# First batch's rows transposed on TensorE, first weights loaded in smaller parts, narrower waits for constants, blank stores moved behind the first turn

## The chip, the cores and the metric

The kernel runs on one core of a Trainium2 chip. The metric is the device time of one execution in microseconds, as the median of several runs. Five engines work side by side, each with its own instruction stream: TensorE (PE; its weight loads are PEld), VectorE (DVE), ScalarE (ACT), GpSimd (POOL) and SyncE (SP), which here mostly issues DMAs. They are ordered among each other only by semaphores that the kernel writes out by hand.

## The reference

For 16 batches of 256 rows of width 512: `x = x + attention(layernorm(x), ctx)`, then `x = x + ffn(layernorm(x))`. The attention is cross attention on 256 context rows of width 256, with 16 query heads and 8 key and value heads of width 128 (`softmax(q k^T / sqrt(128)) v`, then the product with Wo). The ffn works on all 4096 rows at once: a gate picks 4 of 32 experts for a row (2 of 4 groups first), each expert has 128 places and drops what comes after, its output is weighted, and a shared expert (`silu(x Wg) * (x Wu) Wd`) is added for all rows. Everything is float32; the kernel keeps that accuracy by splitting each operand into a float16 high part and a float16 rest and multiplying three times (hi*hi, hi*lo, lo*hi).

## The kernel before, in words

The attention is cut into 128 turns: turn i is batch b = i // 8 and key/value head j = i % 8, which serves two query heads. PE's order is written out in `pe_program`: in turn i it multiplies `scores(i)`, half of `query(i+1)`, `attend(i-1)` (probabilities times values), the other half of `query(i+1)`, `key(i+1)` and `project(i-1)` (product with Wo into ps_out), and in some turns a filler (values of the next batch, gate, rank). So turn 1 is the first with a projection, project(0), at line 1691 with ps_out. After the turns come the experts and the shared expert.

Every product of PE goes through a pair of copies: ACT writes the high half (`query_high`, `key_high`, `value_high`, `head_high`: L905, L899, L912, L1002), then DVE the rest (`query_low`, `key_low`, `value_low`, `head_low`: L1231, L1226, L1237, L1324). Between scores and attend, DVE adds the mask and finds the maxima (`maxima`, L1302), ACT takes the exponentials (`exps`, L989), DVE the scales, POOL and DVE normalise and split them (`probs_high` L734, `probs_low` L1319), and SP turns them by two DMA transposes (`turn_probs`, L570).

Weights are not ready at the start. SP loads them in jobs of up to 512 KB into four staging buffers (`load_weight`, L493); ACT makes the high half (`weight_high`, L893, 128x1024), DVE the rest (`weight_low`, L1170, 128x1024). A buffer is loaded again only after DVE has finished the job before it in that buffer (`next_chunks`). `split_amid` and `split_last` say which jobs are split in which turn, in the middle (behind the maxima) and at the end. A turn takes PE about 9.8 us (project(0) starts at 31.50, project(2) at 51.15 us), and the first turns carry two or three splits each.

The start: SP issues x (two halves), ctx, wk, wq, wv, the mask and two small constants; POOL writes 14 constants (`constants`, L661 to L680), and PE, DVE and ACT all wait for all 14 (`CONSTS`). PE then runs 20 products of zeros (`RAMP`, L1900) to keep itself busy until `key(0)`. Batch 0's layer norm goes DVE statistics (L1174), POOL's inverse deviation (L694), DVE (L1195), ACT's high half (L919), DVE's rest (L1242); SP turns the two row tiles by DMA transpose (L536), and `query(0, h)` waits for both. Behind the transposes on SP stand the next weight loads, the stores of blanks (slot table, blank rows of xn2_rows and of out; L597 to L602) and ctx of batch 1 (L603).

## Time and profile before

| | us |
|---|---|
| median of 3 runs (1606.94 to 1607.52) | 1607.12 |
| the profiled execution, device time | 1609.17 |
| the profiled execution, span of the core | 1607.1 |
| PE busy (share) | 1592.7 (99%) |
| DVE busy | 1221.2 (76%) |
| ACT busy | 843.4 (52%) |
| POOL busy | 787.2 (49%) |
| DMA mean | 137 GB/s |

Matmuls overlap in the profile, so PE's busy time says that it always had one in flight, not that it was at its peak. The start of one matmul to the start of the next is the better measure of its pace.

### The profile page before, as it was taken

What the parts mean: (1) busy time and instruction counts of PE and PEld (TensorE: products, weight loads), DVE (VectorE), ACT (ScalarE), POOL (GpSimd) and SP (SyncE); (2) the same over time, 40 slices, a digit from 0 to 9 for tenths busy, and PEclk for the clock granted to TensorE, in tenths of its full rate; (3) what the DMA queues carried; (4) which work ended last, traced back from release to release, by engine and by line L of the source; (5) the groups of instructions that cost most, each with busy time, mean ns of one, the idle gap of its engine ahead of it and who ended that gap; (6) DMA issues with size and microseconds to landing.
All of it is one profiled execution on the core that took longest, in us unless ns stands there. A gap on an engine that the chain in (4) does not pass through costs nothing. (4 is left out here: it accounts for less than half of the span.)

```text
span 1607.1 us, 36017 instructions
## 1 busy us (share of the span) xinstructions
PE 1592.7 (99%) x12519; PEld 1112.8 (69%) x12519; DVE 1221.2 (76%) x3541; ACT 843.4 (52%) x2086; POOL 787.2 (49%) x1092
## 2 busy tenths in 40 slices
PE   8999999999999999999999999999999999999999
PEld 5666666666666666766666666666677787887876
DVE  7988787878777787878777777878776347776785
ACT  6764544454544554544445454544444156666673
POOL 3444646464555646464645556463536532432432
PEclk9999999999999999999999999999999999999999
DMA  8765445454545454544445444445447658988954
GB/s 256 190 156 120 98 98 109 81 113 80 126 81 126 94 118 97 103 107 100 113 87 126 87 119 100 110 99 104 104 99 260 176 157 244 245 243 261 247 134 95
DMA packets 400243, 219.39 MB, mean 137 GB/s; under 512 B 348464, under 2 KB 356656, under 8 KB 400064
## 3 DMA queue, kind: packets, MB, share of 16 engines
q1 hardware_dynamic: 384176, 191.80, 47.4%
q0 software_dynamic: 15328, 24.25, 8.6%
q8 instruction: 101, 1.65, 0.4%
q10 hardware_dynamic: 560, 1.05, 0.2%
q14 instruction: 78, 0.64, 0.1%
HBM read 92.92 MB, written 40.80 MB: 83 GB/s over the span
## 5 line engine op out<-in xcount | busy, mean ns | idle before, releaser
L989 ACT ACTIVATE arena<-arena,neg_max 128x256 f32<-128x256 f32 x512 | 253.7, 496 | 377.8 <-DVE neg_max L1302 347.5
L734 POOL TENSOR_SCALAR arena<-arena,prob_scale 128x256 f16<-128x256 f32 x384 | 184.6, 497 | 468.5 <-DVE prob_scale L1311 466.4
L1691 PE MATMUL ps_query<-xn_both,arena 128*128 128x256 f16 x1024 | 279.1, 273 | 0.7 <-DMA xn_both<-xn_half 0.7
L1692 PE MATMUL ps_query<-xn_both,arena 128*128 128x256 f16 x1024 | 279.1, 273 | 0.0
L1693 PE MATMUL ps_query<-xn_both,arena 128*128 128x256 f16 x1024 | 279.1, 273 | 0.0
L1302 DVE CUSTOM_DVE_ANT_0 arena<-ps_score,mask_add 128x256 f32<-128x256 f32 x512 | 186.2, 419 | 75.9 <-PE ps_score L1693 74.7
L1319 DVE SCALAR_TENSOR_TENSOR arena<-arena,prob_scale 128x256 f16<-128x256 f32 x384 | 236.3, 664 | 8.5 <-POOL arena L734 8.5
L1691 PE MATMUL ps_out<-arena,o_t 128*128 128x512 f16 x512 | 194.1, 379 | 1.0 <-DVE o_t L1324 1.0
L1692 PE MATMUL ps_out<-arena,o_t 128*128 128x512 f16 x512 | 194.0, 379 | 0.0
L1693 PE MATMUL ps_out<-arena,o_t 128*128 128x512 f16 x512 | 194.0, 379 | 0.0
L1324 DVE SCALAR_TENSOR_TENSOR o_t<-ps_head,o_t 128x512 f16<-128x512 f32 x128 | 88.4, 690 | 97.5 <-ACT o_t L1002 96.0
L784 POOL DMA_INDIRECT slot_table<-entry,slot_at x128 | 130.8, 1022 | 48.0 <-issue 33.8
L1691 PE MATMUL ps_score<-k_both,q_t 128*128 128x256 f16 x512 | 139.5, 272 | 2.8 <-DVE q_t L1231 1.0
L1693 PE MATMUL ps_score<-k_both,q_t 128*128 128x256 f16 x512 | 139.5, 273 | 0.0
L1692 PE MATMUL ps_score<-k_both,q_t 128*128 128x256 f16 x512 | 139.5, 272 | 0.0
L1002 ACT ACTIVATE o_t<-ps_head 128x512 f16<-128x512 f32 x128 | 76.1, 594 | 88.9 <-PE ps_head L1826 65.5
L1691 PEld LDWEIGHTS ps_query<-xn_both,arena 128*128 128x128 f16 x1024 | 100.2, 98 | 26.3 <-DMA xn_both<-xn_half 1.2
L1692 PEld LDWEIGHTS ps_query<-xn_both,arena 128*128 128x128 f16 x1024 | 100.2, 98 | 25.2
L1439 DVE SCALAR_TENSOR_TENSOR arena<-arena 128x1024 f16<-128x1024 f32 x96 | 116.1, 1220 | 0.1
L1693 PEld LDWEIGHTS ps_query<-xn_both,arena 128*128 128x128 f16 x1024 | 100.2, 98 | 11.5
L1014 ACT ACTIVATE arena<-arena 128x1024 f16<-128x1024 f32 x96 | 100.7, 1049 | 2.2 <-PE ps_out L1693 2.2
L742 POOL TENSOR_TENSOR arena<-arena 128x256 f16<-128x256 f32 x128 | 91.7, 717 | 10.7
(343 smaller groups left out, 4175.5 us busy)
## 6 DMA issues: line engine op xcount, KB each, us to landing
arena<-w SPq DMA_DIRECT2D x96, 512.0 KB, 5.4
x_in<-x SPq DMA_DIRECT2D x15, 512.0 KB, 3.7
out_rows_dram<-x SPq DMA_DIRECT2D x30, 256.0 KB, 2.4
xn_rows<-xn_half SPq DMA_DIRECT2D x15, 512.0 KB
out_rows_dram<-weight_in POOLq DMA_DIRECT2D x28, 256.0 KB
x2t_kept<-xn_both SPq DMA_DIRECT2D x12, 512.0 KB, 3.0
ctx_in<-ctx_t SPq DMA_DIRECT2D x16, 256.0 KB, 3.0
weight_in<-wq SPq DMA_DIRECT2D x8, 512.0 KB, 5.0
```

The source lines that it names most:

```text
L734: pool.tensor_scalar(p_rows[:, 0, c, :], probs[:, c, :], prob_scale[:, c:c + 1], 1.0, ALU.mult, ALU.mult).then_inc(norm_hi, 1)
L742: pool.tensor_tensor(p_rows[:, 1, c, :], probs[:, c, :], p_rows[:, 0, c, :], ALU.subtract).then_inc(last_lo, 1)
L784: pool.indirect_dma_start(slot_table, bass.IndirectOffsetOnAxis(ap=slot_at[z % 2][:, t, k:k + 1], axis=0), entry[z % 2][:, t, k, :], None, ...
L989: act.activation(probs[:, c, :], probs[:, c, :], ACT.Exp, bias=neg_max[:, c:c + 1], scale=-1.0, accum_out=prob_sum[:, c:c + 1]).then_inc(e ...
L1014: act.activation(expert_w[e % HELD].hi[:, at], expert_in[e % AHEAD][:, at], ACT.Copy, scale=W_S).then_inc(expert_hi[part], 1)
L1302: dve.tensor_tensor_reduce(out=probs[:, c, :], in0=ps_score[h][:, t * S:(t + 1) * S], in1=mask_add[b % 2][:, :], scale=-SCORE_SCALE, scala ...
L1319: dve.scalar_tensor_tensor(p_rows[:, 1, c, :], probs[:, c, :], prob_scale[:, c:c + 1], p_rows[:, 0, c, :], ALU.mult, ALU.subtract).then_in ...
L1324: dve.scalar_tensor_tensor(o_t.lo, ps_head[:, :], 1.0 / P_S, o_t.hi, ALU.mult, ALU.subtract).then_inc(head_lo, 1)
L1439: dve.scalar_tensor_tensor(expert_w[e % HELD].lo[:, at], expert_in[e % AHEAD][:, at], W_S, expert_w[e % HELD].hi[:, at], ALU.mult, ALU.sub ...
L1691: pe.matmul(dst, a.hi, b.hi, start=start and n == 0, stop=False)
L1692: pe.matmul(dst, a.hi, b.lo, start=False, stop=False)
L1693: m = pe.matmul(dst, a.lo, b.hi, start=False, stop=stop and n == len(pairs) - 1)
```

## The change

`first_transposed(t)` transposes row tile t of batch 0 on PE: 8 transposes of 128x128 against a float16 identity (`ident_first`, a view of o_t that POOL fills, one memset and one select more) into the two score banks as float16. ACT's `first_copy(0)` and DVE's `first_copy(1)` bring them to xn_both. The two DMA transposes of batch 0 go. The first loads are six jobs without a wait: Wq's first two heads in two jobs of 128 columns, Wk's first head of 128 columns, wv, wq chunk 1, the rest of Wk; later jobs move by two in number. ACT waits for 2 constants, PE for 1, 8 and then all, DVE for all only ahead of turn 0, where POOL's memset of xn2_half and minus_half come first. PE runs 16 products of zeros, then 3 and 4 behind the two transposed tiles, then query(0), key(0), value(0,0,0); value(0,0,1) goes behind key(1). ACT and DVE take query(1) and key(1) ahead of the normalising in turn 0, split three jobs (5, 6 and 7) in turn 0 in place of two, and take ctx of batch 1 in turn 1 (POOL) and turn 2 (DVE). SP issues the load of job 7 (wo 0) only after DVE's split of job 5, and ctx(1) and the blank stores behind the probabilities' transposes of turn 0.

```diff
@@ -66,8 +66,8 @@
-RAMP = 20
-RAMP_KEY = 3
+RAMP = 16
+RAMP_TURNED = (3, 4)
@@ -225,6 +225,7 @@
...
         spare_row = sbuf("spare_row", [1])
+        ident_first = o_t.hi[:, 0:P]
@@ -346,7 +349,8 @@
-        CONSTS = 14
+        CONSTS = 16
+        PLAIN_CONSTS = 7
@@ -363,15 +367,18 @@
...
-        jobs = [by_columns("wk", wk_s, wk, KC, 0, 512, 0), by_columns("wq", wq_s, wq, KD, 0, 256, 1),
-                by_columns("wv", wv_s, wv, KC, 0, 512, 2), by_columns("wq", wq_s, wq, KD, 1, 256, 3),
-                by_columns("wq", wq_s, wq, KD, 2, 256, 0), by_rows("wo", wo_s, wo, PAIR, D, 0, 1),
+        rest = slice(HD, 512)
+        jobs = [by_columns("wq_first", wq_s, wq, KD, 0, HD, 1), by_columns("wq_first", wq_s, wq, KD, 1, HD, 1),
+                by_columns("wk_first", wk_s, wk, KC, 0, HD, 0), by_columns("wv", wv_s, wv, KC, 0, 512, 2),
+                by_columns("wq", wq_s, wq, KD, 1, 256, 3),
+                (("wk", 0), wk_s[:, :, rest], rows_of(wk)[:, :, rest], KC, 512 - HD, 0),
+                by_columns("wq", wq_s, wq, KD, 2, 256, 1), by_rows("wo", wo_s, wo, PAIR, D, 0, 0),
                 by_columns("wv", wv_s, wv, KC, 1, 512, 2), by_columns("wq", wq_s, wq, KD, 3, 256, 3),
-                by_rows("wo", wo_s, wo, PAIR, D, 1, 0), by_columns("wk", wk_s, wk, KC, 1, 512, 1)]
+                by_rows("wo", wo_s, wo, PAIR, D, 1, 1), by_columns("wk", wk_s, wk, KC, 1, 512, 0)]
...
@@ -380,10 +387,14 @@
...
+        FIRST_LOADS = 6
+        beside_another = {1: KD * HD, 5: KC * HD}
+
+        split_amid = {0: (6,), 1: (8,), 2: (11,), 3: (14,), 4: (16,), 5: (18,), 6: (20,), 7: (21,), 8: (24,), 9: (26,),
+                      10: (27,)}
+        split_last = {0: (7,), 1: (9, 10), 2: (12, 13), 3: (15,), 4: (17,), 5: (19,), 6: (22, 23), 8: (25,), 10: (28,)}
@@ -391,7 +402,14 @@
...
             _, _, _, rows, cols, buf = jobs[n]
-            return weight_in[buf // 2][:, buf % 2 * 1024:][:, 0:rows * cols].rearrange("p (k n) -> p k n", k=rows)
+            at = buf % 2 * 1024 + beside_another.get(n, 0)
+            return weight_in[buf // 2][:, at:at + rows * cols].rearrange("p (k n) -> p k n", k=rows)
+
+        def weight_landed(n):
+            if n < len(in_begin):
+                return in_begin[n], 16
+            uses_of_it = [m for m in same_buffer(n) if m >= len(in_begin)]
+            return in_weight[jobs[n][5]], 16 * (uses_of_it.index(n) + 1)
@@ -487,10 +505,10 @@
...
             def load_weight(n):
-                earlier_one = [m for m in same_buffer(n) if m < n]
-                if earlier_one:
+                if n >= FIRST_LOADS:
+                    earlier_one = [m for m in same_buffer(n) if m < n]
                     sp.wait_ge(weight_lo, earlier_one[-1] + 1)
-                sp.dma_start(weight_buf(n), jobs[n][2]).then_inc(in_weight[jobs[n][5]], 16)
+                sp.dma_start(weight_buf(n), jobs[n][2]).then_inc(weight_landed(n)[0], 16)
@@ -582,29 +600,28 @@
...
+            def blank_stores():
+                sp.wait_ge(consts, CONSTS)
+                sp.dma_start(slot_table.rearrange("(p e) c -> p (e c)", e=E),
+                             blank[:, :, :].rearrange("p e c -> p (e c)")).then_inc(out_blank, 16)
+                sp.dma_start(xn2_rows[N:N + CAP, :], xn2_half[:, 0, :, :].rearrange("p h d -> p (h d)")).then_inc(out_blank, 16)
+                for n in range(2):
+                    sp.dma_start(out[N + n * CAP:N + (n + 1) * CAP, :],
+                                 xn2_half[:, 0, :, :].rearrange("p h d -> p (h d)").bitcast(F32)).then_inc(out_blank, 16)
...
             load_x(0)
+            for n in range(2):
+                load_weight(n)
             load_ctx(0)
-            for n in range(3):
+            for n in range(2, FIRST_LOADS):
...
             sp.dma_start(bias_row[:, :], gate_bias.broadcast_to([P, E])).then_inc(in_const, 16)
-            for t in range(TB):
-                turn_xn(0, t)
-            load_weight(3)
-            next_chunks((0, 1, 2))
...
-            load_ctx(1)
-
+            next_chunks((1, 3, 4, 5))
...
                 b, j = divmod(i, KV)
-                next_chunks(split_last.get(i - 1, ()) if i else (3,))
+                next_chunks(split_last.get(i - 1, ()))
@@ -617,6 +634,9 @@
...
                 turn_probs(i)
+                if i == 0:
+                    load_ctx(1)
+                    blank_stores()
@@ -658,13 +678,16 @@
...
             def constants():
+                pool.memset(xn2_half[:, 0, :, :], 0.0).then_inc(consts, 1)
+                pool.memset(minus_half[:, :], -0.5).then_inc(consts, 1)
+                pool.memset(ident_first, 0.0).then_inc(consts, 1)
...
                 pool.memset(lower[:, :, :], 1.0).then_inc(consts, 1)
-                pool.memset(xn2_half[:, 0, :, :], 0.0).then_inc(consts, 1)
                 pool.memset(blank[:, :, 1], 0).then_inc(consts, 1)
-                pool.memset(minus_half[:, :], -0.5).then_inc(consts, 1)
-                pool.wait_ge(consts, 6)
+                pool.wait_ge(consts, PLAIN_CONSTS)
+                pool.affine_select(out=ident_first, in_=ident_first, compare_op=ALU.not_equal, fill=1.0, base=0,
+                                   pattern=[[-1, P]], channel_multiplier=1).then_inc(consts, 1)
@@ -818,7 +841,7 @@
...
                 probs_high(i)
-                if i == 0:
+                if i == 1:
@@ -889,7 +912,7 @@
...
             def weight_high(n):
-                act.wait_ge(in_weight[jobs[n][5]], 16 * (same_buffer(n).index(n) + 1))
+                act.wait_ge(*weight_landed(n))
@@ -926,6 +949,11 @@
...
+
+            def first_copy(t):
+                act.wait_ge(pe_first, t + 1)
+                act.activation(xn_both[0][:, :, :, t * P:(t + 1) * P], ps_last[t].rearrange("p (h k c) -> p h k c", h=2, k=KD),
+                               ACT.Copy, scale=1.0).then_inc(first_copied, 1)
@@ -1054,27 +1082,30 @@
...
-            act.wait_ge(consts, CONSTS)
+            act.wait_ge(consts, 2)
...
                 xn_high(0, t)
-            for n in (0, 1):
+            weight_high(0)
+            first_copy(0)
+            for n in (1, 2, 3):
                 weight_high(n)
+            query_high(0)
             key_high(0)
-            weight_high(2)
-            query_high(0)
-            weight_high(3)
+            for n in (4, 5):
+                weight_high(n)
+            act.wait_ge(consts, CONSTS)
...
                 if i == 0:
-                    for n in split_amid[0]:
-                        weight_high(n)
+                    value_high(ps_fill[0], 0, 0, 0)
...
                 if i == 0:
-                    value_high(ps_fill[1], 0, 0, 0)
+                    query_high(1)
+                    key_high(1)
@@ -1084,15 +1115,17 @@
                 if i == 0:
+                    for n in split_amid[0]:
+                        weight_high(n)
...
@@ -1262,6 +1295,11 @@
...
+            def first_copy(t):
+                dve.wait_ge(pe_first, t + 1)
+                dve.tensor_copy(xn_both[0][:, :, :, t * P:(t + 1) * P], ps_last[t].rearrange(
+                    "p (h k c) -> p h k c", h=2, k=KD)).then_inc(first_copied, 1)
@@ -1485,23 +1523,25 @@
...
-            dve.wait_ge(consts, CONSTS)
...
                 xn_rest(0, t)
+            weight_low(0)
+            first_copy(1)
+            weight_low(1)
             ctx_low(0)
-            for n in (0, 1):
+            for n in (2, 3):
                 weight_low(n)
+            query_low(0)
...
                 value_scaled, 1)
+            weight_low(4)
             dve.wait_ge(value_scaled, 1)
-            weight_low(2)
-            query_low(0)
-            weight_low(3)
+            dve.wait_ge(consts, CONSTS)
@@ -1511,7 +1551,10 @@
...
                     maxima(i)
-                for n in split_amid.get(i, ()):
+                if i == 0:
+                    weight_low(5)
+                    value_low(ps_fill[0], 0, 0, 0)
+                for n in split_amid.get(i, ()) if i else ():
@@ -1542,7 +1585,8 @@
...
                 if i == 0:
-                    value_low(ps_fill[1], 0, 0, 0)
+                    query_low(1)
+                    key_low(1)
@@ -1552,16 +1596,13 @@
...
-                if i == 0:
-                    query_low(i + 1)
-                    key_low(i + 1)
@@ -1571,7 +1612,10 @@
...
                 if i == 0:
+                    for n in split_amid[0]:
+                        weight_low(n)
                     value_low(ps_fill[0], 0, 0, 1)
+                if i == 2:
@@ -1695,11 +1739,14 @@
...
                 b, g = divmod(i, KV)
-                if h == 0:
-                    pe.wait_ge(xt_turned, 16 * TB * (b + 1))
-                    pe.wait_ge(weight_lo, prepared["wq", g])
-                    if i:
-                        pe.wait_ge(query_lo, i)
+                if i == 0:
+                    pe.wait_ge(first_copied, TB)
+                    pe.wait_ge(weight_lo, prepared["wq_first", h])
+                elif h == 0:
+                    if b:
+                        pe.wait_ge(xt_turned, 16 * TB * b)
+                    pe.wait_ge(weight_lo, prepared["wq", g] if g else prepared["wq_first", 1])
+                    pe.wait_ge(query_lo, i)
@@ -1709,7 +1756,7 @@
...
                 pe.wait_ge(ctx_lo, b + 1)
-                pe.wait_ge(weight_lo, prepared["wk", g // 4])
+                pe.wait_ge(weight_lo, prepared["wk", g // 4] if i else prepared["wk_first", 0])
@@ -1720,6 +1767,13 @@
...
+
+            def first_transposed(t):
+                pe.wait_ge(xn_lo, t + 1)
+                for n in range(2 * KD):
+                    h, k = divmod(n, KD)
+                    m = pe.transpose(ps_last[t][:, n * P:(n + 1) * P], xn_half[:, t, h, k * P:(k + 1) * P], ident_first)
+                m.then_inc(pe_first, 1)
@@ -1894,24 +1948,28 @@
...
-            pe.wait_ge(consts, CONSTS)
+            def ramp(count):
+                for _ in range(count):
+                    pe.matmul(ps_out[0][:, :], zeros[:, 0:P], zeros, start=True, stop=True)
+
+            pe.wait_ge(consts, 1)
             zeros = xn2_half[:, 0, 0, :]
-            for _ in range(RAMP):
-                pe.matmul(ps_out[0][:, :], zeros[:, 0:P], zeros, start=True, stop=True)
-            key(0)
-            for _ in range(RAMP_KEY):
-                pe.matmul(ps_out[0][:, :], zeros[:, 0:P], zeros, start=True, stop=True)
+            ramp(RAMP)
+            pe.wait_ge(consts, PLAIN_CONSTS + 1)
+            for t in range(TB):
+                first_transposed(t)
+                ramp(RAMP_TURNED[t])
...
                 query(0, h)
+            key(0)
+            pe.wait_ge(consts, CONSTS)
...
                 if i == 0:
-                    filler(("value", 0, 0, 0), ps_fill[1])
+                    filler(("value", 0, 0, 0), ps_fill[0])
...
                     scores(i)
-                if i == 0:
-                    filler(("value", 0, 0, 1), ps_fill[0])
@@ -1926,6 +1984,8 @@
...
                     key(i + 1)
+                if i == 0:
+                    filler(("value", 0, 0, 1), ps_fill[0])
```

## Rows read from the trace of the kernel before

**Rows 1.** Waits of PE from 31 us on: total us, times, longest.
```profile
PE ps_out L1691 <- DVE o_t L1324: 1.0, 3, 0.6
```
**Rows 2.** Busy time by stretch: PE, PEld, DVE, ACT, POOL; PEclk, DMA share, GB/s.
```profile
31.40:60.00 28.60, 28.50 (x191) 18.57 (x192) 27.20 (x63) 21.13 (x48) 15.48 (x20) 1.00 0.84 237
...
400.00:1190.00 790.00, 788.47 (x5713) 534.03 (x5712) 625.44 (x2052) 392.89 (x1124) 423.88 (x624) 1.00 0.48 104
```
**Rows 3.** Timeline of the start: start us, us, engine, line, operation [idle before <-releaser].
```profile
3.72 1.28 DVE L1174 BATCH_NORM_STATS2 stats<-x_in 128x6 f32<-128x512 f32 x2 [3.72 <-POOL blank L680]
...
3.74 6.70 PE L1900 MATMUL ps_out<-xn_half 128*128 128x512 f16 x20 [3.74 <-POOL blank L680]
...
6.51 0.95 DVE L1195 TENSOR_SCALAR x<-x_in,mean_var,rstd 128x512 f32<-128x512 f32 x1 [1.22 <-POOL rstd L694]
...
8.15 1.29 DVE L1242 SCALAR_TENSOR_TENSOR xn_half<-x,xn_half 128x512 f16<-128x512 f32 x2 [0.24 <-ACT xn_half L919]
...
8.87 2.72 SPq L536 DMA_TRANSPOSE xn_both<-xn_half  x2
...
11.33 0.27 PE L1691 MATMUL ps_fill<-ctx_both,arena 128*128 128x256 f16 x1 [0.89 <-DVE arena L1170]
...
13.49 0.28 PE L1691 MATMUL ps_query<-xn_both,arena 128*128 128x256 f16 x1 [0.70 <-DMA xn_both<-xn_half]
```
**Rows 4.** Loads issued at 0.81, 11.64 and 12.84 us: KB, us from issue to landing.
```profile
x_in<-x SPq DMA_DIRECT2D x1, 256.0 KB, 2.6
...
weight_in<-wq SPq DMA_DIRECT2D x1, 512.0 KB, 3.8
...
weight_in<-wo SPq DMA_DIRECT2D x1, 512.0 KB, 6.4
```
**Rows 5.** Timeline of turns 0 and 1.
```profile
16.32 0.60 ACT L905 ACTIVATE q_t<-ps_query 128x512 f16<-128x512 f32 x1 [2.81 <-PE ps_query L1693]
...
17.70 0.28 PE L1691 MATMUL ps_score<-k_both,q_t 128*128 128x256 f16 x1
...
19.04 0.42 DVE L1302 CUSTOM_DVE_ANT_0 arena<-ps_score,mask_add 128x256 f32<-128x256 f32 x1
...
25.02 0.27 PE L1691 MATMUL ps_score<-k_both,q_t 128*128 128x256 f16 x1 [1.04 <-DVE q_t L1231]
...
26.50 1.21 DVE L1170 SCALAR_TENSOR_TENSOR arena<-weight_in,arena 128x1024 f16<-128x1024 f32 x1
...
27.64 0.41 DVE L1302 CUSTOM_DVE_ANT_0 arena<-ps_score,mask_add 128x256 f32<-128x256 f32 x1
...
30.75 0.69 DVE L1324 SCALAR_TENSOR_TENSOR o_t<-ps_head,o_t 128x512 f16<-128x512 f32 x1 [0.17 <-ACT o_t L1002]
...
31.50 0.39 PE L1691 MATMUL ps_out<-arena,o_t 128*128 128x512 f16 x1 [0.16 <-DVE o_t L1324]
```
**Rows 6.** By line: ns min/median/max, first and last start; one row of the timeline.
```profile
L1021 ACT ACTIVATE xn_both<-ps_fill x32: 1001/1012/1024, 1294.1 to 1573.0; 128x1024 f16<-128x1024 f16 x32
...
L1170 DVE SCALAR_TENSOR_TENSOR arena<-weight_in,arena x20: 1209/1215/1418, 10.0 to 85.7; 128x1024 f16<-128x1024 f32 x20
...
L1216 DVE TENSOR_SCALAR weight_in<-x,mean_var,rstd x4: 531/540/628, 1146.7 to 1211.5; 128x512 f32<-128x512 f32 x4
...
1214.76 1.06 PE L1728 MATMUL ps_score<-blank,xn_half 128*128 128x128 f16 x16
```
**Rows 7.** Turn 3 in the timeline, and DVE's waits for PE from 31 to 110 us.
```profile
49.92 0.69 DVE L1324 SCALAR_TENSOR_TENSOR o_t<-ps_head,o_t 128x512 f16<-128x512 f32 x1
...
51.15 0.38 PE L1691 MATMUL ps_out<-arena,o_t 128*128 128x512 f16 x1
...
DVE arena L1302 <- PE ps_score L1693: 2.0, 2, 1.3
```
**Rows 8.** Busy time by stretch within the products of zeros, columns as in Rows 2.
```profile
3.70:8.30 4.60, 4.56 (x11) 1.64 (x12) 3.08 (x7) 1.01 (x3) 1.53 (x3) 1.00 1.01 339
8.30:10.50 2.20, 2.14 (x10) 0.78 (x8) 2.20 (x4) 2.20 (x3) 0.00 (x0) 1.00 0.60 168
```

More of the change, by code:

```diff
@@ L307, in build @@
         in_weight = [signal(f"in_weight{n}") for n in range(4)]
+        in_begin = [signal(f"in_begin{n}") for n in range(3)]
+        pe_first, first_copied = signal("pe_first"), signal("first_copied")
         xt_turned, x2t_turned, out_rows, out_xn2, in_table = (signal(n) for n in ("xt_turned", "x2t_turned", "out_rows", "out_xn2", "in_table"))
@@ L381, in build @@
         prepared = {job[0]: n + 1 for n, job in enumerate(jobs)}
-        split_amid = {0: (4,), 1: (6,), 2: (9,), 3: (12,), 4: (14,), 5: (16,), 6: (18,), 7: (19,), 8: (22,), 9: (24,),
-                      10: (25,)}
-        split_last = {0: (5,), 1: (7, 8), 2: (10, 11), 3: (13,), 4: (15,), 5: (17,), 6: (20, 21), 8: (23,), 10: (26,)}
-        assert sorted(n for table in (split_amid, split_last) for ns in table.values() for n in ns) == list(range(4, JOBS))
+        FIRST_LOADS = 6
[3 more added lines that the diff above has]
+        split_last = {0: (7,), 1: (9, 10), 2: (12, 13), 3: (15,), 4: (17,), 5: (19,), 6: (22, 23), 8: (25,), 10: (28,)}
+        assert sorted(n for table in (split_amid, split_last) for ns in table.values() for n in ns) == list(
+            range(FIRST_LOADS, JOBS))
         def same_buffer(n):
@@ L415, in build @@
         before = {}
-        for bank_no, first_use in ((0, [("value", 0, 0, 1)]), (1, [("key", 0), ("value", 0, 0, 0)])):
+        for bank_no, first_use in ((0, [("value", 0, 0, 0), ("value", 0, 0, 1)]), (1, [("key", 0)])):
             held = list(first_use)
@@ L591, in sync_program @@
             sp.dma_start(bias_row[:, :], gate_bias.broadcast_to([P, E])).then_inc(in_const, 16)
-            for t in range(TB):
-                turn_xn(0, t)
-            load_weight(3)
-            next_chunks((0, 1, 2))
-            sp.wait_ge(consts, CONSTS)
-            sp.dma_start(slot_table.rearrange("(p e) c -> p (e c)", e=E),
-                         blank[:, :, :].rearrange("p e c -> p (e c)")).then_inc(out_blank, 16)
-            sp.dma_start(xn2_rows[N:N + CAP, :], xn2_half[:, 0, :, :].rearrange("p h d -> p (h d)")).then_inc(out_blank, 16)
-            for n in range(2):
-                sp.dma_start(out[N + n * CAP:N + (n + 1) * CAP, :],
-                             xn2_half[:, 0, :, :].rearrange("p h d -> p (h d)").bitcast(F32)).then_inc(out_blank, 16)
-            load_ctx(1)
+            next_chunks((1, 3, 4, 5))
             for i in range(TURNS):
                 b, j = divmod(i, KV)
-                next_chunks(split_last.get(i - 1, ()) if i else (3,))
+                next_chunks(split_last.get(i - 1, ()))
                 if j == 1 and b + 1 < B:
@@ L1563, in dve_program @@
                 early_key = live and second(b, j) is not None and second(b, j)[0] == "value"
-                if i + 1 < TURNS and early_key:
+                if 0 < i < TURNS - 1 and early_key:
                     key_low(i + 1)
```

10 lines of the change are left out of this document (5 added, 5 removed).

## The prediction

> **What bounds the kernel now.** I read the waits of PE first, then the busy time by stretch, then the timeline of the first 52 us. PE is the bound from its first projection on: between 400 and 1190 us it is busy for 788.47 of 790 us [rows 2], and from 31 us to the end its largest wait, for o_t, sums to 1.0 us in three places [rows 1]. So the end moves by what project(0), at 31.50 us [rows 5], moves, less any new stall behind it. What lies ahead of 31.50 is a start-up whose waits aren't covered. PE begins real work with key(0) at 11.33 and query(0) at 13.49 [rows 3]. A product of 256 columns starts every 0.109 us, one of 512 every 0.216, so PE's own work up to project(0) is 16.33 us: key and query(0) 3.27, two values 2.6, two scores 2.62, query(1) 2.62, key(1) 0.65, query(2) 2.62, attend(0) 1.3, key(2) 0.65. From 11.33 to 31.50 it takes 20.17, so 3.84 us are holes (1.5 ahead of query(0), filled with three products of zeros, 1.2 ahead of scores(1), the rest small).
>
> DVE is the hidden second bound. From 26.50 to 31.50 its instructions stand back to back, with 0.17 us of idle [rows 5], and between 31.4 and 60 it is busy for 27.20 of 28.60 [rows 2]. project(0) waits for DVE's o_t (30.75 + 0.69), that for ACT behind exps(1), and exps(1) for maxima(1) at 27.64 [rows 5]. Moving PE's start alone would thus be worth nothing; DVE's chain must move too.
>
> **The change part by part.** All times are of the profiled execution.
>
> Constants. DVE's statistics waited for POOL's last constant at 3.72 [rows 3]; the first half of x had landed at 0.81 + 2.6 = 3.4 [rows 4], but the second, issued 0.46 later and 0.3 slower, only at about 4.2, where DVE stood at 4.3 anyway. The wait was nearly hidden: worth 0.1. POOL's two more constants (about 0.4, ending at 4.1) lie ahead of the statistics' end at 5.2, so they cost nothing; without that cover, 0.4. PE starts its zeros at about 1.8 and ends them near 7.5; its wait for x follows.
>
> Layer norm. DVE's first L1195 took 0.95 beside POOL's split of ctx, where the same shape otherwise takes 0.54 [rows 3, 6]. ctx now comes behind two weight loads, at about 7.8, so I take 0.54. The normalised rows end at 6.9 and 7.4, ACT's high halves at 7.6 and 8.1, DVE's rests at 8.3 and 8.9 (0.61 apart, as in [rows 3]).
>
> Transposes. Removed: 8.87 to 13.49, that is two issues of 1.36 one after the other and the landing [rows 3]. Added: 8 transposes per tile, 0.45 us (16 stand in 0.89 [rows 6]); tile 0 from 8.4, the zeros behind it 0.64, tile 1 from 9.5 to 10.0. ACT's copy takes 1.01 [rows 6] and ends at 10.0. DVE's copy of 128x1024 float16 out of PSUM has no row. The nearest are 1.22 for a two-input operation with 1024 elements and 0.54 for a one-input one with 512 [rows 6]; I take 1.2 by equal element count and keep 0.6 as the lower end. It runs from 10.15 to 11.35, so query(0) starts at 11.42, against 13.49. ACT's splits of 512 and 256 elements lie beside it, and all the small loads have landed by then.
>
> The Trainium skill, "VectorE: DVE Perf Modes", section "Why PSUM operands drop a tier", says that an operand in PSUM still allows two 16-bit elements a cycle in a one-input operation. By that rule the copy takes about 0.6 (an estimate) and the sum ends 0.55 us lower. No row here shows it.
>
> Turn 0, from query(0) at 11.42. Query ends at 14.04, key(0) at 14.7 (ctx and Wk's head are split at 12.9), value(0,0,0) at 16.0 (wv split by DVE at 14.1). ACT and DVE bring q_t and k_t as before, 0.3 and 0.6 us behind PE's last product [rows 5]: ready at 15.96, hidden by the value, so scores(0) starts at 16.0 against 17.70. DVE's split of job 4 ends at 17.45, which holds query(1) by 0.2, and maxima(0) start at 17.4 against 19.04. Then DVE: maxima 1.38, job 5 (768 elements) 0.87, value 0.67, scales 0.45, done at 20.65; q_t and k_t of turn 1 follow ACT, which follows PE's query(1) at 20.1 and key(1) at 20.8: ready at 22.0. PE covers this with value(0,0,1) until 22.07, so scores(1) starts at 22.07 against 25.02. DVE goes on with three rests of the probabilities to 23.35, job 6 (1.14) to 24.5, value to 25.2, job 7 (1.14) to 26.35. The chain from query(0) to maxima(1) has no slack of DVE over 0.7 us: maxima(1) start at 26.35 against 27.64. PE does query(2) from 24.6 (held 1.2 by job 6's split), attend(0) at 26.15 and its last third at 27.45 (the probabilities' second transpose), and ends key(2) at 29.86.
>
> Turn 1, as before from maxima(1): exps(1) end at 28.8, o_t's high half at 29.4, DVE's rest at 29.42 + 0.69, project(0) at 30.16. PE's own account gives the same: 16.33 of work and 2.4 of holes from 11.42. **Gain at project(0): 1.34.**
>
> Job 7 (wo 0) was loaded at 12.84 and now waits for the split of job 5, so it is issued at 19.7. With 3.8 us on a quiet queue, as the load at 11.64 had [rows 4], it lands at 23.5, is split by ACT by 24.6 and costs nothing. The margin is 0.7 us.
>
> Turns 1 to 3. ctx(1), the blank stores (0.8 MB) and ctx's splits stood under start-up holes of SP and in turn 0 of DVE. On SP they now stand ahead of the load of wo 1, which is issued at 28.3 instead of 26.93; it lands near 32.3, and ACT wants it by 32.65. DVE's ctx split (0.61) moves from turn 0 to turn 2. So DVE is 1.34 ahead in turns 1 and 2 but 0.73 in turn 3, while PE is 1.34 ahead. There o_t was ready at 49.92 + 0.69 and used at 51.15, slack 0.54 [rows 7]: 0.61 of it goes, and PE stalls by about 0.1. Later DVE waits for PE twice, up to 1.3 us [rows 7], so it catches up and nothing more is lost. Wait for a late wo 1: 0 to 0.8, taken as 0.1.
>
> **Sum.** 1.34 - 0.1 - 0.1 = 1.1 us. The profiled span of 1607.1 goes to 1606.0; the median of the runs shown is 1607.12, equal to that span though the profiled execution's device time was 1609.17, so I take the same 1.1 off the median: 1606.0.
>
> **The rivals.**
> Rival 1, the copy is fast: everything from query(0) on starts 0.55 earlier, 1605.5. For it, the row with one input is fast for its size [rows 6]; against it, that row is from SBUF. This is the page's rule, above.
>
> Rival 2, the weights come late and it ends slower than before. The place is the load of wo 0 and, behind it, wo 1. Their landing times range from 3.8 to 6.4 [rows 4]. Landing of wo 0 after 19.7 + 5.7 = 25.4 puts maxima(1) behind 27.64 (1.05 for ACT, 1.14 for DVE, and hand-overs), and the gain is gone; at 6.4 it is 26.1, project(0) at 32.2, and the time 1607.9. For it: no cover left on DVE. Against: only one other load (wq 3, issued at 17.5) is under way then.
>
> Rival 3, the clock. In the first 4.60 us of zeros 11 products of 512 columns start (0.42 us each, the lower level, 1.2 GHz), in the next 2.20 us 10 (0.22, the upper, 2.4 GHz) [rows 8]. PE then held the upper level through holes of 0.9 and 0.7 us [rows 3]. Now there is a hole of 0.9 ahead of the transposes, and transposes with zeros in place of key(0). If the lower level is granted there, transposes and zeros take 1.4 more up to query(0), and query(0) 2.6 more: 1606.0 + 4.0 = 1610.0. Against it: the 16 transposes at 1214.76 ran 0.056 apart, the upper level [rows 6], though between dense products.
>
> The Trainium skill, "TensorE: Matmul & The Clock Gate", section "Part 4: PE-mode transpose", says that the full clock doesn't engage for transposes, since they don't count as busy in the same way. By that rule rival 3 would be likely; the trace agrees only that they can run at the upper level.
>
> Rival 4, the stall is hidden anyway: DVE stays as late as before through its added split in turn 0, PE only waits longer for o_t, and the time is 1607.1. For it: DVE's work in turn 0 grows by 0.87 (job 5) less 0.61 (ctx). Against: its chain starts 1.64 earlier.
>
> **How the numbers follow.** Forecast 0.43 (1605.6 to 1606.5), rival 1 0.20, rival 2 0.12, rival 3 0.06, rival 4 0.15, and 0.04 for a gain beyond this: with no hole at all and the fast copy, project(0) would come at 27.2 and the time be 1602.8. About 0.2% (3.2 us) is what a measurement of this kernel can tell from no change. Nearly every case lies within it: same 0.92, faster 0.03, slower 0.05. The range is 1604.6 to 1607.9; it holds all but parts of rival 3, the large gain and a late load.
>
> **What would show it.** Right: query(0) near 11.4 with its transposes 0.056 apart; scores(0) near 16.0 and scores(1) near 22.1; maxima(1) near 26.4; project(0) near 30.2; a stall of about 0.1 at project(2). L1170 for wo 0 without idle time ahead of it. Wrong: transposes 0.107 apart (rival 3), DVE idle ahead of job 7 or 10 (rival 2), maxima(1) at 27.6 (rival 4), a DVE copy of 0.6 (rival 1), or PE stalls behind turn 3 larger than before.

## The result and the profile after

The changed kernel takes 1611.67 us (median of 9 runs, 1610.38 to 1613.86) against 1607.21 for the kernel before in the same comparison (9 runs): a ratio of 1.0028, 95% interval 1.002 to 1.0037. It is slower, by about 4.5 us, where 1.1 us of gain was forecast. The profiled execution took 1612.24 us with a span of 1610.4, which is 3.3 more than the 1607.1 of before. The rest of the 4.5 didn't come back: in later comparisons the kernel before took 1608.83 to 1609.27 and the changed one 1611.89, so the loss to be explained is 3.1 to 3.3 us.

The start came nearly as forecast. L1775 are the transposes on TensorE, L955 and L1300 the two copies. This is the timeline of the changed kernel up to project(0) (start us, us, engine, line, operation, idle before and releaser):

```profile
1.81 5.48 PE L1953 MATMUL ps_out<-xn_half 128*128 128x512 f16 x16 [1.81 <-POOL minus_half L682]
...
6.43 1.00 DVE L1228 TENSOR_SCALAR x<-x_in,mean_var,rstd 128x512 f32<-128x512 f32 x2 [1.22 <-POOL rstd L717]
...
8.92 0.61 PE L1775 MATMUL ps_score<-o_t,xn_half 128*128 128x128 f16 x8 [1.63 <-DVE xn_half L1275]
...
9.56 1.02 ACT L955 ACTIVATE xn_both<-ps_score 128x1024 f16<-128x1024 f16 x1 [0.88 <-PE ps_score L1775]
...
10.01 0.61 PE L1775 MATMUL ps_score<-o_t,xn_half 128*128 128x128 f16 x8
...
10.65 0.69 DVE L1300 COPY xn_both<-ps_score 128x1024 f16<-128x1024 f16 x1 [0.68 <-PE ps_score L1775]
...
11.40 0.28 PE L1735 MATMUL ps_query<-xn_both,arena 128*128 128x256 f16 x1
...
16.03 0.27 PE L1735 MATMUL ps_score<-k_both,q_t 128*128 128x256 f16 x1
...
25.02 0.28 PE L1735 MATMUL ps_query<-xn_both,arena 128*128 128x256 f16 x1 [1.36 <-DVE arena L1203]
...
26.68 0.41 DVE L1340 CUSTOM_DVE_ANT_0 arena<-ps_score,mask_add 128x256 f32<-128x256 f32 x1
...
30.54 0.39 PE L1735 MATMUL ps_out<-arena,o_t 128*128 128x512 f16 x1 [0.60 <-DVE o_t L1362]
```

project(0) is 0.96 us earlier than the 31.50 of [rows 5]. The loss lies behind it. Busy time by stretch (PE, PEld, DVE, ACT, POOL; granted clock, DMA share, GB/s), the same stretches as [rows 2]:

```profile
31.40:60.00 28.60, 24.52 (x166) 15.81 (x165) 24.55 (x57) 17.15 (x37) 10.51 (x17) 1.00 0.85 218
400.00:1190.00 790.00, 788.81 (x5717) 535.20 (x5716) 627.79 (x2049) 396.05 (x1125) 427.05 (x626) 1.00 0.49 104
```

Between 400 and 1190 us nothing differs. Between 31.4 and 60 PE is busy for 24.52 us instead of 28.50, so 3.98 us go missing there. Two holes hold them, shown in PE's timeline:

```profile
38.23 0.38 PE L1875 MATMUL ps_head<-arena 128*128 128x512 f16 x1 [2.31 <-DMA arena<-arena]
54.49 0.39 PE L1735 MATMUL ps_out<-arena,o_t 128*128 128x512 f16 x1 [1.77 <-DVE o_t L1362]
```

The first is attend(1), which waits for SP's transposes of the probabilities of turn 1. The second is project(2). Before, neither wait existed [rows 1, 7]. The waits between 28 and 110 us (total, times, longest) tell what is behind the second:

```profile
ACT arena L916 <- DMA weight_in<-wq: 4.4, 1, 4.4
...
DVE arena L1203 <- ACT arena L916: 2.6, 2, 2.0
...
PE ps_out L1735 <- DVE o_t L1362: 2.4, 2, 1.8
PE ps_head L1875 <- DMA arena<-arena: 2.3, 1, 2.3
ACT arena L916 <- DMA weight_in<-wo: 2.0, 1, 2.0
```

ACT waits 4.4 us for one load of Wq (columns of turn 5, job 14); DVE, which works in order, can't go on to turn 2's o_t without it. SP's timeline tells why this load and the transposes are late. First the kernel before:

```profile
24.28 2.60 SPq L570 DMA_TRANSPOSE arena<-arena  x2
26.93 0.58 SPq L493 DMA_DIRECT2D weight_in<-wo  x1
...
32.85 2.85 SPq L570 DMA_TRANSPOSE arena<-arena  x2
35.76 0.57 SPq L493 DMA_DIRECT2D weight_in<-wq  x1
36.38 0.53 SPq L493 DMA_DIRECT2D weight_in<-wo  x1
36.95 0.47 SPq L493 DMA_DIRECT2D weight_in<-wq  x1
41.58 3.05 SPq L570 DMA_TRANSPOSE arena<-arena  x2
```

And the changed one:

```profile
22.77 2.73 SPq L588 DMA_TRANSPOSE arena<-arena  x2
25.54 0.58 SPq L532 DMA_DIRECT2D ctx_in<-ctx_t  x1
26.17 0.48 SPq L605 DMA_DIRECT2D slot_table<-blank  x1
26.68 0.43 SPq L607 DMA_DIRECT2D xn_rows<-xn_half  x1
...
28.14 0.54 SPq L511 DMA_DIRECT2D weight_in<-wo  x1
...
31.88 5.03 SPq L588 DMA_TRANSPOSE arena<-arena  x2
...
41.28 3.66 SPq L588 DMA_TRANSPOSE arena<-arena  x2
45.00 1.62 SPq L511 DMA_DIRECT2D weight_in<-wq  x2
```

Two things are to be seen. The two transposes of turn 1 begin at 31.88, earlier than before, but take 5.03 us to issue instead of 2.85, behind ctx(1), the blank stores and the loads queued after them. I call this cause Q (queue). And the third load of turn 2, issued at 36.95 before, is now issued at 45.00, behind the transposes of turn 2. A buffer is loaded again only after DVE has split the job before it there. The change exchanges buffers 0 and 1 for the first twelve jobs, while the later ones keep theirs. Before, that Wq load took the buffer of wo 1, split at the end of turn 1; now it takes the buffer of Wk's second half, split in the middle of turn 2. Wo's chunk for turn 3 took that late buffer before, where it did no harm, since it is split at the end of turn 3, and the Wq load already in the middle of it. I call this cause B (buffers).

### The profile page after: what moved, and what is told of

The parts are those of the page before. It is cut to its first block, busy times and chain, and to the rows that moved or that the text cites. A ratio compares the mean times of both kernels' runs of the same rounds, so it can differ in the third digit from the quotient of the medians.

```text
span 1610.4 us, 36059 instructions
## 1 busy us (share of the span) xinstructions
PE 1593.2 (99%) x12535; PEld 1113.9 (69%) x12535; DVE 1226.9 (76%) x3544; ACT 849.5 (53%) x2089; POOL 789.0 (49%) x1094
## 4 chain that ended last, share of the span: by engine, by line
PE 92%; DVE 2%; DMA 2%; issue 1%; SPq 1%; POOL 1%; ACT 0%; POOLq 0%; DVEq 0%
PE ps_query L1735 8%; PE ps_query L1737 8%; PE ps_query L1736 8%; PE ps_fill L1737 7%; PE ps_fill L1736 7%; PE ps_fill L1735 7%; PE ps_out L1735 7%; PE ps_out L1736 7%; PE ps_out L1737 7%; PE ps_score L1735 5%; PE ps_score L1737 5%; PE ps_score L1736 5%; PE ps_head L1880 3%; PE ps_head L1875 3%; PE ps_head L1876 3%; PE ps_fill L1902 1%
## 5 line engine op out<-in xcount | busy, mean ns | idle before, releaser
L807 POOL DMA_INDIRECT slot_table<-entry,slot_at x128 | 130.2, 1017 | 48.0 <-issue 33.8
L1875 PE MATMUL ps_head<-arena 128*128 128x512 f16 x256 | 96.9, 378 | 2.3 <-DMA arena<-arena 2.3
```

The source lines that it names most:

```text
L807: pool.indirect_dma_start(slot_table, bass.IndirectOffsetOnAxis(ap=slot_at[z % 2][:, t, k:k + 1], axis=0), entry[z % 2][:, t, k, :], None, ...
L1875: pe.matmul(ps_heads, v.hi, p_t[s].hi, start=s == 0, stop=False)
```

## The experiments

What the runs are compared by, beside the ratio, is the start of project(i) in the profiled execution less that of the kernel before, in us:

| run | project(0) | (1) | (2) | (3) | end | ratio to before (95%) |
|---|---|---|---|---|---|---|
| the change | -0.96 | +1.40 | +3.34 | +3.45 | +3.26 | 1.0028 (1.002 to 1.0037) |
| e12, the change again | -0.99 | +1.44 | +2.43 | +2.54 | +3.57 | 1.0018 (1.0008 to 1.0027) |
| e1 blank stores early | -0.35 | -0.46 | +1.88 | +3.58 | +3.74 | 1.0015 (1.0006 to 1.0024) |
| e2 buffers as before | -1.29 | +2.44 | +2.44 | +2.44 | +4.05 | 1.0015 (1.0006 to 1.0024) |
| e3 both | -0.12 | -0.23 | +0.23 | +0.34 | -0.37 | 1.0006 (0.9997 to 1.0015) |
| e4 before, blanks late | -0.04 | +0.83 | +0.83 | +0.83 | +0.26 | 1.0007 (0.9998 to 1.0016) |
| e5 both, ctx(1) early too | +1.06 | +0.96 | +1.42 | +1.53 | +1.86 | 1.0016 (1.0007 to 1.0025) |
| e6 buffers, blanks in turn 4 | -1.42 | -1.53 | -1.26 | -1.10 | +0.24 | 0.9997 (0.9988 to 1.0006) |
| e11, the same again | -1.25 | -1.33 | -1.11 | -0.13 | +0.14 | 0.9997 (0.9988 to 1.0006) |
| e7 e6, rows turned by DMA | +3.50 | +3.70 | +3.70 | +3.84 | +4.18 | 1.0037 (1.0023 to 1.005) |
| e8 e6, all constants waited for | +0.10 | +0.21 | +0.67 | +0.78 | +0.65 | 1.0004 (0.9995 to 1.0014) |
| e9 blanks in turn 4 alone | -1.53 | -1.63 | +0.67 | +0.87 | +0.76 | 1.0011 (1.0002 to 1.0021) |
| e10 before, buffers exchanged | +0.31 | +0.28 | +2.64 | +2.75 | +3.16 | 1.0018 (1.0009 to 1.0027) |

One profiled execution is good to about 1 us here: the change and e12 are one kernel and differ by 0.9 at project(3), e6 and e11 by 1.0 (e11 has one more wait of 0.71 at attend(3) for turned probabilities). Ratios of about 1.0015 with intervals of 0.0009 to each side can hardly be told from one another, so the waits in the traces carry the argument on the single causes. The times forecast for the first runs were set against 1607.2, while the kernel before took 1609.05 beside e1 to e4.

**e1, the blank stores ahead of wo 0.** Undoes most of Q alone.

```diff
-            next_chunks((1, 3, 4, 5))
+            next_chunks((1, 3, 4))
+            blank_stores()
+            next_chunks((5,))
...
                 if i == 0:
                     load_ctx(1)
-                    blank_stores()
```

> The changed kernel with one thing undone: the blank stores (0.8 MB) are issued in the start-up again, ahead of the load of wo 0; ctx of batch 1 stays behind the transposes of turn 0. Theory Q (queue): the stores, issued at 26.2 to 28.1 us, push the loads behind them, and these the probabilities' transposes of turn 1, for which attend(1) waits 2.31 us. 0.8 MB at 350 GB/s is 2.3 us, so that wait falls to under 0.5 and the time to 1609.0 to 1610.0. Theory B (buffers): the stall comes from the staging buffers' exchange; the wait at attend(1) stays above 1.5 and the time within 0.5 of 1611.7.

The wait at attend(1) is gone, as theory Q has it; the time of 1611.88 is above its forecast. For project(0) keeps only 0.35 of its gain, and project(2) waits 1.96 (B, untouched). Then the clock falls: project(3) comes another 1.70 late. Busy time by stretch in e1:

```profile
51.00:53.00 2.00, 0.07 (x1) 0.00 (x0) 1.90 (x8) 1.41 (x5) 0.66 (x2) 1.00 0.00 0
53.00:55.00 2.00, 1.97 (x8) 0.84 (x9) 2.00 (x4) 2.00 (x5) 1.92 (x4) 0.79 0.00 0
55.00:57.00 2.00, 2.00 (x6) 0.68 (x5) 2.00 (x4) 1.01 (x2) 1.71 (x4) 0.50 0.68 129
```

After 2 us in which PE is busy for 0.07, the granted clock falls to 0.50 (1.2 of 2.4 GHz) for the work that follows. In this execution the hole cost more than its length.

**e2, the buffers exchanged back.** Undoes B alone: in the first twelve jobs 0 and 1 change places, as in the kernel before.

```diff
-        jobs = [by_columns("wq_first", wq_s, wq, KD, 0, HD, 1), ...
+        jobs = [by_columns("wq_first", wq_s, wq, KD, 0, HD, 0), ...
```

> The changed kernel with staging buffers 0 and 1 exchanged for the first twelve jobs, so that wo 1 lies in buffer 0 and Wk's second half in buffer 1, as before the change. Theory B: wq chunk 5 (buffer 0) is loaded again at the start of turn 2 and not behind its transposes; ACT's wait of 4.4 us for it in turn 3 and DVE's of 2.0 go, and PE's stall of 1.77 at project(2) falls to under 0.5: 1609.5 to 1610.3. Theory Q: project(2) is late only because attend(1) was; exchanging buffers changes nothing, 1611.7 within 0.5.

ACT's wait of 4.4 for wq and the wait at project(2) go, as theory B has it; the one at attend(1) stays, at 2.01. The time, 1611.09, is above the forecast. Yet project(1) moves by 3.73 from project(0), since here too the clock falls after the hole:

```profile
35.00:37.00 2.00, 0.59 (x6) 0.28 (x3) 2.00 (x8) 1.68 (x4) 0.24 (x1) 1.00 1.18 198
...
39.00:41.00 2.00, 2.00 (x11) 1.37 (x10) 1.03 (x3) 0.99 (x2) 1.72 (x5) 0.50 0.95 319
```

So 1.7 of e2's 3.73 are clock (3.73 - 2.01). The changed kernel itself had a hole of 2.31 (2.38 in e12) at the same place and its clock stayed at 1.00 in both profiled executions. Of all fourteen profiles only e1, e2 and e7 show a 2 us stretch below 0.99. The fall of the clock doesn't explain why undoing one cause alone brought so little in the medians: the mean granted clock of a whole execution is 0.999 in 2 of e1's 11 executions and in 3 of e2's 11, and 1.000 in the others, whose medians are 1611.01 and 1611.03. It is 0.999 in 3 of the first 9 executions of the changed kernel too, in 3 of e10's 11 and in none of e12's 10.

**e3, both together,** the edits of e1 and e2:

```diff
+            blank_stores()
...
+        jobs = [by_columns("wq_first", wq_s, wq, KD, 0, HD, 0), ...
```

> Both edits: blank stores in the start-up and the first twelve jobs' buffers exchanged. If theories Q and B each hold a part, both stalls go and only the gain of 0.96 at project(0) is left, less small waits: 1606.0 to 1607.0, faster than the kernel before by 0.2 to 1.2. If only Q holds: as the first run of this call. If only B: as the second.

Both waits go, the span (1606.7) lies in the forecast and the ratio's interval holds 1. But the start gain, which the forecast kept, is lost: project(0) comes at 31.38. In the timeline of e3 ACT waits for wo 0 (issued at 19.83 behind the blank stores):

```profile
25.28 2.00 ACT L917 ACTIVATE arena<-weight_in 128x1024 f16<-128x1024 f32 x2 [2.42 <-DMA weight_in<-wo]
```

**e4, the kernel before with its blank stores behind turn 0's transposes.** Q's main part alone, nothing else of the change.

```diff
-            [the four blank stores, in the start-up]
...
                 turn_probs(i)
+                if i == 0:
+                    [the four blank stores]
```

> The kernel before with one part of the change alone: the blank stores are issued behind the probabilities' transposes of turn 0 (ctx of batch 1 stays where it was). Theory Q: the loads of turn 1 and the transposes of turn 1 land later; PE waits 1 to 2 us at attend(1): 1608.0 to 1609.5. Theory B: no buffer changes, so nothing happens: 1607.2 within 0.3.

A wait of 0.82 appears at attend(1), under the 1 to 2 us expected, and project(1) to project(3) come 0.83 later, at full clock:

```profile
37.66 0.38 PE L1822 MATMUL ps_head<-arena 128*128 128x512 f16 x1 [0.82 <-DMA arena<-arena]
```

This isolates the blank stores' part in Q. It is smaller than 2.31. Two things differ from the changed kernel, and no run tells them apart: ctx(1) isn't in the queue here, and the transposes of turn 1 begin at 32.80 and not at 31.88 (they take 3.46 to issue). The ratio doesn't tell it from no change.

**e5, e3 with ctx(1) early too,** so that nothing of the change's late traffic is left.

```diff
             next_chunks((1, 3, 4))
+            load_ctx(1)
             blank_stores()
```

> As the version with both edits (blank stores in the start-up, first twelve jobs' buffers exchanged), but ctx of batch 1 is loaded in the start-up too, ahead of the stores. Theory Q: 0.25 MB less stands ahead of turn 1's loads; but 1.05 MB now stand ahead of wo 0, which already held maxima(1): project(0) comes at 31.4 to 31.9 against 31.50 before the change, no stall in turns 1 to 3, span 1606.9 to 1607.6. Rival (the start-up's gain is real whatever the stores do): project(0) at 30.2 to 30.5 and span near 1606.

Worse than e3, and than expected (project(0) at 32.56 against 31.4 to 31.9): ACT waits 3.5 for wo 0, attend(0) waits 1.54 for its turned probabilities, project(0) is 1.06 later than before. The place in front of wo 0 isn't free at all: wo 0 is issued at 20.69 and lands 5.8 later, against 19.75 and 3.7 in the changed kernel.

**e6, buffers as before and the blank stores behind turn 4's transposes.**

```diff
                 if i == 0:
                     load_ctx(1)
+                if i == 4:
                     blank_stores()
```

> The changed kernel with the first twelve jobs' buffers exchanged and the blank stores issued behind the transposes of turn 4 (ctx of batch 1 behind those of turn 0). Theory Q: nothing stands ahead of wo 0 or of turn 1's loads but ctx; project(0) stays at 30.2 to 30.5, the wait at attend(1) is under 0.3, project(3) is 0.8 to 1.3 us earlier than in the kernel before, and the span is 1605.8 to 1606.4: faster than before by 0.05 to 0.08%. Rival (ctx of batch 1 alone is enough to delay the transposes of turn 1): attend(1) waits over 1 us and the span is 1607 or more.

Both holes are gone with the start gain kept, as expected: -1.42 at project(0), -1.10 at project(3). The span was forecast at 1605.8 to 1606.4 and is 1607.3; this is taken up at the end. SP's timeline of e6, against that of the changed kernel:

```profile
31.41 2.61 SPq L588 DMA_TRANSPOSE arena<-arena  x2
34.08 0.57 SPq L511 DMA_DIRECT2D weight_in<-wq  x1
34.70 0.52 SPq L511 DMA_DIRECT2D weight_in<-wo  x1
35.27 0.47 SPq L511 DMA_DIRECT2D weight_in<-wq  x1
```

The transposes take 2.61 again, and job 14 is issued at 35.27, not 45.00. Against before the median is 1608.66 to 1609.27, which is no difference that can be told.

**e9, the blank stores in turn 4 with the change's buffers,** and **e10, the kernel before with buffers 0 and 1 exchanged in its ten written-out jobs.** These two isolate B.

```diff
                 if i == 0:
                     load_ctx(1)
+                if i == 4:
                     blank_stores()
```

```diff
-        jobs = [by_columns("wk", wk_s, wk, KC, 0, 512, 0), by_columns("wq", wq_s, wq, KD, 0, 256, 1),
+        jobs = [by_columns("wk", wk_s, wk, KC, 0, 512, 1), by_columns("wq", wq_s, wq, KD, 0, 256, 0),
...
```

> The changed kernel with the blank stores issued behind turn 4's transposes and its own buffers kept (wo 1 in buffer 1, Wk's second half in buffer 0). Theory Q predicts no wait at attend(1); theory B predicts that the late load of wq chunk 5 still holds project(2) and project(3): 1.8 to 3.5 us together, so project(3) at +0.7 to +2.5 against the kernel before. If B were only a consequence of the queue's delay, project(3) would be at -1.1 as in the version with exchanged buffers.

> The kernel before with one part of the change alone: staging buffers 0 and 1 exchanged for the first ten jobs, the later ones as they were. Theory B: wq chunk 5 is loaded behind turn 2's transposes, ACT waits 4 to 5 us for it in turn 3 and PE is later by 2.5 to 3.7 us from project(3) on; ratio 1.0015 to 1.0023. Rival (the order of buffers costs only where the start-up is early already): under 0.5 us.

In e9 there is no wait at attend(1), although ctx(1) still stands there, so Q doesn't come about without the blank stores. From project(1) to project(2) it loses 2.30. SP's timeline of e9 shows both, quick transposes in turn 1 and the late Wq load:

```profile
31.32 2.63 SPq L588 DMA_TRANSPOSE arena<-arena  x2
...
42.95 1.25 SPq L511 DMA_DIRECT2D weight_in<-wq  x2
```

In e10 six buffer numbers of the kernel before are changed and nothing else, and it gets slower, at 1.0018: project(1) stands at +0.28, project(2) at +2.64. Both runs came as theory B expected. e10's waits between 28 and 110 us:

```profile
ACT arena L893 <- DMA weight_in<-wq: 4.8, 1, 4.8
...
PE ps_out L1691 <- DVE o_t L1324: 2.4, 2, 2.2
```

and its SP, with the load issued behind the transposes of turn 2 as in the changed kernel:

```profile
41.89 3.19 SPq L570 DMA_TRANSPOSE arena<-arena  x2
45.13 1.14 SPq L493 DMA_DIRECT2D weight_in<-wq  x2
```

**e7, e6 with batch 0's rows turned by DMA as before.** It leaves the rest of the change (small loads, order, zeros behind) as it is.

```diff
-                first_transposed(t)
...
+            for t in range(TB):
+                turn_xn(0, t)
```

> The version with the blank stores in turn 4, with one part undone: batch 0's rows are turned by two DMA transposes again, not by TensorE; products of zeros stay. If the transposes on TensorE are what moved the start, query(0) comes about 2 us later, at 13.2 to 13.6, but key(0) stands behind it now, so scores(0) at 17.9 to 18.2 and project(0) at 31.8 to 32.3: span 1607.4 to 1608. If the reordering of turn 0 (query(1) and key(1) ahead of the normalising) is what moved project(0), it stays within 0.3 of the version with TensorE: 30.2 to 30.7.

```profile
14.50 0.40 PE L1735 MATMUL ps_query<-xn_both,arena 128*128 128x256 f16 x1 [5.00 <-DMA xn_both<-xn_half]
```

query(0) starts 3.56 later than e6's 10.94, and project(0) 4.92 later. The 1.36 between them is the clock: after the hole of 5.00 the granted clock is 0.50 from 14.5 to 16.5, and query(0) runs at 0.21 us a product for its first twelve. So the transposes on TensorE are worth 3.6 here, and the clock that stays up with them 1.4. The first is more than expected (query(0) at 13.2 to 13.6) and the second wasn't foreseen. They hold for this order of the start only: with all the first loads queued ahead of them, the two DMA transposes took 4.11 us to issue (from 8.30), against 2.72 in [rows 3], and key(0) doesn't cover the wait.

**e8, e6 with PE, DVE and ACT waiting for all constants.**

```diff
-            act.wait_ge(consts, 2)
+            act.wait_ge(consts, CONSTS)
...
+            dve.wait_ge(consts, CONSTS)
...
-            pe.wait_ge(consts, 1)
+            pe.wait_ge(consts, CONSTS)
```

> The version with the blank stores in turn 4, with one part undone: DVE, ACT and PE wait for all constants before their first work, as before the change. My account of the start says this wait was worth 0.1 us; POOL now ends the constants at 4.07 and the statistics started at 3.60, so they start 0.5 later and all behind them up to 0.4: project(0) 0.3 to 0.5 later. Rival: the wait is hidden by the second half of x, which lands at 4.2: no difference over 0.1 at query(0).

PE's timeline of e8:

```profile
4.12 6.02 PE L1955 MATMUL ps_out<-xn_half 128*128 128x512 f16 x16 [4.12 <-POOL blank L704]
9.98 0.61 PE L1777 MATMUL ps_score<-o_t,xn_half 128*128 128x128 f16 x8
```

In e6 the zeros start at 1.81 and the transposes at 8.46. project(0) is 1.52 later, where 0.3 to 0.5 was expected. DVE's rests start only 0.50 later (8.12 against 7.62). The larger part is PE's: its 16 products of zeros stand in line ahead of the transposes, and they start when PE's wait ends. This is read from the trace; the three waits weren't widened one by one.

**e11 and e12, e6 and the change once more,** measured beside e9 and e10 on the same chip.

> The version with exchanged buffers and blank stores in turn 4 once more. Its first run had project(3) 1.10 us earlier than the kernel before but a ratio of 0.9997 (0.9988 to 1.0006) and a span equal to the one before within 0.3. If the gain of 1.1 lasts to the end, the ratio is 0.9990 to 0.9996; if it is regularly given back late (in the last turns and at the experts), 0.9998 to 1.0002. Project(0) at 30.0 to 30.5 either way.

> The changed kernel once more, on the same chip as the versions of this call. Theories Q and B: the waits are at the same places, attend(1) 1.8 to 2.8 us and project(2) 1.3 to 2.3, project(3) 3 to 4 us later than before the change. If these waits were chance, one of them is missing.

The change is slower again (1611.89 against 1608.83), e11 is the same again (1608.51, between the two cases of its forecast). The wait at attend(1) came back in e12, at 2.38. The one at project(2) came back at less than expected:

```profile
53.58 0.39 PE L1735 MATMUL ps_out<-arena,o_t 128*128 128x512 f16 x1 [0.82 <-DVE o_t L1362]
```

The load of job 14 was issued at 45.02 (45.00 in the first profile) but landed after 3.7 us and not 4.6, and ACT waited 3.44 for it. So B's size changes from one execution to the next by about 1 us.

These four runs give the parts by medians of one chip too: e12 1611.89, e9 (no Q) 1610.49, e11 (neither) 1608.51. That is 1.4 for Q and 2.0 for B, against 2.5 and 1.6 by the traces below. The whole (e12) and B in the kernel before (e10) are clear of the noise, since their intervals lie above e11's. Q alone isn't, by medians: the intervals of e12 and e9 overlap.

## Why the prediction was wrong

**The step that failed is "Turns 1 to 3".** It took 0.1 for a stall at project(2) and 0.1 for a late wo 1. Measured there are 2.31 at attend(1) and 1.77 at project(2), 4.08 in all, which covers the 3.98 us that PE's busy time lacks. The forecast of -1.1 and the measured +3.3 of the span differ by 4.4: 3.9 from this step (4.08 - 0.2), 0.4 from the start (0.96 in place of 1.34), and 0.1 of rounding and the rest. The prediction took 0.2% (3.2 us) as the least that can be told from no change; the intervals are 0.0009 (1.4 us) to each side, so this loss can be told.

Its first error was to follow the displaced traffic to the weights behind it on SP and not to the transposes. ctx(1) and the blank stores were priced by wo 1 alone: issued at 28.3 (28.14 measured), landing at 32.3 (28.14 + 5.7 = 33.8 measured), ACT late by up to 0.8 (2.0 measured). The probabilities' transposes of turn 1 stand on the same queue behind all of it, and PE's attend(1) waits for them. No step named them. e4 gives it alone, at a third of its size (0.82 in the kernel before); e9 takes it away by moving the blank stores only.

Its second error was a sentence of the diff read too fast: later jobs "move by two in number". The buffer numbers of the first twelve jobs were exchanged too, so that which job frees a buffer for which changed at the seam to the later ones. With it the load of job 14 falls behind a DVE split of the middle of turn 2, and so behind turn 2's transposes on SP. The "split_amid" table shown in the change would have told it. e10 gives it alone: 2.36 between project(1) and project(2), 1.0018 in time.

**The sum of the parts, by the traces.** From project(0) to project(1) the change loses 2.36 where e6 gains 0.11: Q is 2.5. From project(1) to project(3) it loses 2.05 where e6 loses 0.43, and e9 and e10 lose 2.50 and 2.47: B is 1.6 in the changed kernel (2.05 - 0.43), 2.1 in e9 and 2.5 in e10, which is compared with the kernel before itself. Q and B of the changed kernel make the 4.1 us of the two waits. By e12's trace B is 0.7 (1.10 - 0.43), so these parts are good to about 1 us.

**The rivals.** Rival 2 came nearest: late weights, and slower than before. Its price of 1607.9 was worked out for wo 0 and was far too low, and wo 0 was on time: issued at 19.75, landed 3.7 later, as the forecast had it (19.7 and 3.8). Its other place, wo 1, was late: ACT waited 2.02 for it and DVE stood idle for 0.60 ahead of its split (job 10), one of the prediction's signs of being wrong. But no wait of PE in the changed kernel ends with wo 1; the late weight that held PE was Wq's job 14, which the rival didn't name. Where e3 really makes wo 0 late, by 2.42 at ACT, project(0) comes at 31.38, so the rival's path was a true one. Rival 4 is refuted: maxima(1) came at 26.68.

**The start, point by point.** query(0) at 11.40 (11.42 forecast), scores(0) 16.03 (16.0), maxima(0) 17.39 (17.4), scores(1) 22.19 (22.07), the hold at query(2) 1.36 (1.2), maxima(1) 26.68 (26.35), project(0) 30.54 (30.16). The 11.42 was hit by luck, by two errors of opposite sign: the transposes started at 8.92 and not at 8.4, since DVE's first rest took 1.10 (7.67 to 8.77; 0.69 in e1, e6 and e9), and DVE's copy took 0.69 and not 1.2. In e1, e3 and e6 they started near 8.46, and e6's query(0) at 10.94. So rival 1's mechanism was the true one. The Trainium skill, "VectorE: DVE Perf Modes", section "Why PSUM operands drop a tier", was right in this: its rule gave an estimate of about 0.6 for two 16-bit elements a cycle out of PSUM, and the trace agrees with 0.69 for 128x1024 float16. My 1.2 took the element count of a two-input row with float32.

**Rival 3, the clock.** It didn't come: the transposes stood 0.056 us apart (8 within the 0.61 of their row), the upper level, with a granted clock of 1.00. The spacing is the better witness, for the granted clock reads 1.00 also in the first line of [rows 8], where the zeros stood 0.42 apart. The Trainium skill, "TensorE: Matmul & The Clock Gate", section "Part 4: PE-mode transpose", says that the full clock doesn't engage for transposes; the trace doesn't agree for 8 of them with products of zeros before and between. What I gave no chance to was a fall of the clock behind a new hole in turns 1 to 3, which e1 and e2 show.

**Constants.** Priced at 0.1 by DVE alone. e8 measures 1.5 at project(0) when all three waits are widened, through PE's zeros. The prediction took the early zeros as given in the step of the transposes, so the total wasn't wrong by it, but the share was.

**What stays open.** The prediction also took it that the end moves by what project(0) moves, less any new stall. In e6 and e11 the kernel is 1.1 to 1.5 us ahead at project(1) and 0.1 to 0.2 behind at the end. The ground is lost in small steps over the 128 turns and behind them: e6 stands at -0.9 at project(96), -0.3 at project(127) and 0.0 at the experts. I didn't settle what takes it. So even without the two stalls the forecast of 1606.0 isn't shown to have been within reach: e6 and e11 are 0.6 and 0.3 us below the kernel before by medians, no difference that can be told. Nor did I settle why the clock fell after holes of 1.96 and 2.01 in e1 and e2, and not after 2.31 and 2.38 in the two profiles of the changed kernel.

## What to carry to other kernels

When work on an in-order DMA queue is moved, list every instruction behind the new place up to the next idle stretch of that queue, and follow the consumers of each, the transposes of the main loop first; "off the start-up path" is not "off the path". When jobs with rotating buffers are renumbered or renamed, write down for each load which earlier job frees its buffer and when, also at the seam to the jobs that the diff doesn't touch. A new hole of about 2 us in TensorE cost its length, and in two of the six profiles that had one of 1.9 to 2.4 us in the turns it cost 1.7 more at the lower clock.

## What the runs showed of the hardware

- The two DMA transposes of a turn's probabilities took 2.60 to 2.85 us to issue in turns 0 and 1 of the kernel before, and 5.03 in turn 1 of the changed one, with 1 MB of ctx and stores and the loads of wo, wk, x and the mask issued in the 6 us ahead of them. With the blank stores taken from there (e9) they took 2.63.
- DVE's float16 copy of 128x1024 out of PSUM took 0.69, ACT's 1.02.
- After holes the granted clock fell to 0.50 in three profiles: in e1 after a wait of 1.96, in e2 after 2.01, in e7 after 5.00. It cost 1.70, 1.7 and 1.4 us. After waits of 2.31 and 2.38 at the place of e2's, in two executions of the changed kernel, and of 1.92 in e9 and 2.20 in e10 at the place of e1's, it stayed at 1.00.
